# Turning x's tokens with VectorE block transpositions and a DRAM round trip instead of TensorE transposes, in a two-direction Mamba-2 layer

## The reference, cut to what matters

```python
def _mamba2(x, Win, convw, convb, dtb, Alog, Dsk, normw, Wout):
    z, xBC, dt = jnp.split(x @ Win, [D_INNER, D_INNER + CONV_CH], axis=-1)      # 512 | 640 | 8
    xBC = _silu(depthwise causal convolution over 4 tokens of xBC + convb)
    xs, Bm, Cm = jnp.split(xBC, [D_INNER, D_INNER + NGROUPS * D_STATE], axis=-1) # 512 | 64 | 64
    xs = xs.reshape(b, l, NHEADS, HEADDIM)                                       # 8 heads of 64
    dt = jax.nn.softplus(dt + dtb)
    dA = jnp.exp(dt * -jnp.exp(Alog))
    # over the tokens: h = dA_t * h + dt_t * x_t (outer) B_t ;  y_t = C_t . h
    y = ys + Dsk * xs
    y = y * _silu(z)
    y = y * jax.lax.rsqrt(jnp.mean(y * y, axis=-1, keepdims=True) + 1e-05) * normw
    return y @ Wout

def reference(...):
    out = concat(_mamba2(layernorm(x), f...), flip(_mamba2(flip(layernorm(x)), b...))) @ Wo + bo
    x = x + out
    return x + (layernorm(x) @ W.T + b + (layernorm(x) @ V_r) @ C.T)
```

## Time and profile before

| | |
|---|---|
| median of 3 runs | 630.85 us (628.61 to 631.13) |
| span of the profiled execution | 629.0 us |
| median minus that span | 1.85 us |
| PE, DVE, ACT, POOL busy | 592.0, 503.6, 547.2, 409.4 us |
| one period (forward plus reversed scan), seven times | 73.6 us |
| opening up to the first period; after the last | 90.8 us; 23.0 us |

### The profile page before, as it was taken

How to read it: one execution, slowest core, us unless ns; L and a number is a source line. 1 busy time by engine, 2 the same in 40 slices (tenths; PEclk the granted TensorE clock), 3 DMA queues, 4 the chain that set the end, 5 groups by cost and what they waited for, 6 DMA issues and landing times.

```text
span 629.0 us, 13895 instructions
## 1 busy us (share of the span) xinstructions
PE 592.0 (94%) x4320; PEld 461.0 (73%) x4320; DVE 503.6 (80%) x991; ACT 547.2 (87%) x1197; POOL 409.4 (65%) x427
## 2 busy tenths in 40 slices
PE   1998999999999999999999999999999999999995
PEld 1776687777877777777877778777777777777784
DVE  2669788996979879797888969798797978879663
ACT  4689998979999899988999799897999989997952
POOL 1006948787486864878476874868648684768843
PEclk9999999999999999999999999999999999999997
DMA  7533514236061541418132360614416170343500
GB/s 220 189 109 115 198 40 124 92 106 203 8 200 27 171 114 41 169 28 255 28 116 95 107 204 0 211 25 160 126 28 182 26 241 12 92 122 99 181 1 33
DMA packets 43545, 70.71 MB, mean 112 GB/s; under 512 B 8000, under 2 KB 30592, under 8 KB 43520
## 3 DMA queue, kind: packets, MB, share of 16 engines
q1 hardware_dynamic: 43520, 70.40, 36.7%
HBM read 59.37 MB, written 4.72 MB: 102 GB/s over the span
## 4 chain that ended last, share of the span: by engine, by line
PE 55%; ACT 18%; DVE 13%; issue 8%; POOL 3%; SPq 1%; DMA 1%; DVEq 0%; ACTq 0%; POOLq 0%
PE mi L621 14%; ACT bs L968 8%; PE pj L487 7%; PE py L580 7%; PE pj L489 6%; PE pj L488 6%; DVE xc L1378 5%; PE mi L687 4%; PE py L598 3%; ACT bs L974 2%; ACT L953 2%; DVE bs L1405 2%; DVE ss L1437 2%; ACT xc L935 1%; DVE xres L1445 1%
## 5 line engine op out<-in xcount | busy, mean ns | idle before, releaser
L1378 DVE SCALAR_TENSOR_TENSOR xc<-pj,cw,xc 128x510 f32<-128x510 f32 (+2 forms) x240 | 175.4, 744 | 24.9 <-ACT xc L935 23.0
L968 ACT ACTIVATE bs<-bs,s_all 128x128 f32<-128x128 f32 x512 | 158.4, 388 | 0.2
L1892 POOL TENSOR_TENSOR yg<-yg,sz 128x512 f32<-128x512 f32 x60 | 76.9, 1287 | 81.6 <-DVE yg L1424 81.6
L487 PE MATMUL pj<-xnt_hi,w_hi 128*128 128x512 f32 x288 | 126.1, 438 | 0.9 <-DVE xc L1378 0.8
L489 PE MATMUL pj<-xnt_hi,w_lo 128*128 128x512 f32 x288 | 114.2, 396 | 0.0
L488 PE MATMUL pj<-xnt_lo,w_hi 128*128 128x512 f32 x288 | 113.8, 395 | 0.0
L621 PE MATMUL mi<-wc,yg 128*128 128x256 f32 x480 | 112.1, 386 | 0.8 <-DVE xres L1445 0.2
L621 PEld LDWEIGHTS mi<-wc,yg 128*128 128x128 f32 x480 | 88.6, 190 | 16.9 <-issue 3.3
L1405 DVE TENSOR_TENSOR bs<-bs,gm 128x512 f32<-128x512 f32 x128 | 86.1, 680 | 8.5 <-ACT bs L974 7.7
L1871 POOL TENSOR_TENSOR xw<-xdt,w_end 128x512 f32<-128x512 f32 x48 | 49.6, 1045 | 49.8 <-ACT w_end L953 40.9
L1390 DVE TENSOR_TENSOR xdt<-mi,dt 128x512 f32<-128x512 f32 x64 | 42.8, 688 | 44.6 <-PE mi L547 44.2
(11 more groups left out here) (149 smaller groups left out, 1021.6 us busy)
## 6 DMA issues: line engine op xcount, KB each, us to landing
bs<-rows_dram SPq DMA_DIRECT2D x64, 512.0 KB, 5.4
es<-rows_dram SPq DMA_DIRECT2D x128, 96.0 KB, 3.0
xres<-in_x SPq DMA_DIRECT2D x8, 512.0 KB, 3.6
cc<-bcm SPq DMA_DIRECT2D x32, 128.0 KB, 2.3
out<-ot SPq DMA_DIRECT2D x32, 128.0 KB, 3.4
xin<-in_x SPq DMA_DIRECT2D x7, 512.0 KB, 5.3
rows_dram<-s_rows SPq DMA_DIRECT2D x128, 4.0 KB
cz<-bcm SPq DMA_DIRECT2D x16, 128.0 KB, 2.4
```

The lines of the kernel that those rows point to most:

```text
L487: pe.matmul(ps[:], hi(k), xnt_hi[:, k, :], start=(k == 0), stop=False)
L968: i = nc.scalar.activation(bs[:, h, Q * c:Q * c + Q], bs[:, h, Q * c:Q * c + Q], ACT.Relu, bias=s_all[:, d, 0, c, h:h + 1], scale=-1.0)
L1378: i = dve.scalar_tensor_tensor(xc[:, t, to], pj[bank][:, of], cw[:, d, t, KW - 1 - s:KW - s], xc[:, t, to], ALU.mult, ALU.add)
L1892: pool.tensor_tensor(yg[:, d, p, :], yg[:, d, p, :], sz[:, d, p, :], ALU.mult).then_inc(yg_ready, 1)
```

## The change

1. `x_tokens` goes, on TensorE (256 transposes of 128x128) and on VectorE, and with it 64 entries of the tables that share the two `mi` banks.
2. VectorE gets `turn`: for each of the four x tiles of a scan one block transposition of 128x512, which turns each 32x32 block inside its group of 32 partitions and writes to a new buffer `turned`. `xw` now lies in `turned`'s storage.
3. SP gets `scatter` (four DMAs per scan, from `turned` to DRAM, in runs of 2 KB) and `gather` (four per scan, one for each chunk, from DRAM, in runs of 512 B, into `yg`'s storage for that direction). `scatter` waits for all four `turn`s, the first `gather` for all four `scatter`s and for the last head pair of the scan before.
4. VectorE gets `step` in place of its part of `x_tokens`: two instructions of 128x256 per chunk, with both operands (`tok` and `dt`) in SBUF. `intra` of the first pair waits for all four steps; `decayed_x` of a chunk waits for its step.
5. `s_all` is stored by heads, so that `put_rows` and `put_decays` are one DMA each instead of four, and `repeat_decays` is four DMAs per scan instead of eight.
6. The orders of all five lists are new, opening and last scan included.

```diff
+SQ = 32
+BLK = P // SQ
...
+LOOP = ["1bt", "a0", "a1", "dtm", "1s0", "1s1", "0ss", "dtt", "1s2", "0o0", "0o1", "0S", "0ST", "0bt", "1ss", "1o0",
+        "0s0", "0s1", "1o1", "0s2", "1S", "t0", "1ST", "f0", "t1", "t2", "f1", "t3", "f2", "f3"]
...
-        xw = sb("xw", [P, NC - 1, DI])
+        turned = sb("turned", [P, BLK, NC, KI, SQ])
+        xw = turned[:].rearrange("p b c t r -> p (b c t r)")[:, 0:(NC - 1) * DI].rearrange("p (j n) -> p j n", j=NC - 1)
...
+        tok = [yg[:, d].rearrange("p a (b c r) -> p (a b c r)", b=BLK, r=SQ).rearrange("p (b c t r) -> p b c t r", b=BLK, c=NC, t=KI)
+               for d in range(2)]
...
+        tok_dram = nc.dram_tensor("tok_dram", (2, P, BLK, DI), F32, kind="Internal").ap()
...
-                for c in range(NC):
-                    sp.dma_start(rows_dram[d, 0, :, Q * c:Q * c + Q], s_rows[NH * c:NH * c + NH, d, 0, :]).then_inc(rows_stored, 16)
+                sp.dma_start(rows_dram[d, 0].rearrange("h (c q) -> (h c) q", c=NC), s_rows[:, d, 0, :]).then_inc(rows_stored, 16)
+
+            def scatter(b, d):
+                sp.wait_ge(turn_ready, KI * (2 * b + d + 1))
+                alone(sp)
+                for i in range(BLK):
+                    sp.dma_start(tok_dram[d, :, i].rearrange("(q r) n -> r q n", q=BLK),
+                                 turned[SQ * i:SQ * i + SQ].rearrange("r q c t n -> r q (c t n)")).then_inc(tok_stored, 16)
+
+            def gather(b, d, j):
+                if j == 0:
+                    sp.wait_ge(tok_stored, 16 * BLK * (2 * b + d + 1))
+                    alone(sp)
+                    pair_done(b, d, KI - 1)
+                c = ORDER[d][j]
+                sp.dma_start(tok[d][:, :, c].rearrange("p b t n -> p b (t n)"),
+                             tok_dram[d].rearrange("p b (c n) -> p b c n", c=NC)[:, :, c]).then_inc(tok_loaded[j], 16)
...
-            def x_tokens(phase, it, d, j):
-
-                ps, free = misc(phase, it, f"{d}x{j}")
+            def turn(b, d, t):
+
+                u = 2 * b + d
+                dve.wait_ge(xs_ready, KI * u + t + 1)
+                dve.transpose(turned[:, :, :, t, :].rearrange("p b c r -> p c b r"), xs[:, d, t, :]).then_inc(turn_ready, 1)
+
+            def step(b, d, j):
+
+                dve.wait_ge(tok_loaded[j], 16 * (2 * b + d + 1))
+                if j == 0:
+                    dve.wait_ge(dt_ready[d], b + 1)
                 c = ORDER[d][j]
-                dve.tensor_tensor(xdt[:, c, :].rearrange("p (h q) -> p h q", h=NH), ps[:].rearrange("p (h q) -> p h q", h=NH),
-                                  dt[:, d, c, :].unsqueeze(2).broadcast_to([P, NH, HP]), ALU.mult).then_inc(free, 1)
+                of = tok[d][:, :, c].rearrange("p (z a) t r -> p z a t r", z=2)
+                to = xdt[:, c, :].rearrange("p (t z a r) -> p z a t r", z=2, a=2, r=SQ)
+                by = dt[:, d, c, :].rearrange("p (t z) -> p z t", z=2)
+                for z in range(2):
+                    i = dve.tensor_tensor(to[:, z], of[:, z], by[:, z].unsqueeze(1).unsqueeze(3).broadcast_to([P, 2, KI, SQ]), ALU.mult)
+                i.then_inc(step_ready, 1)
```

More of the change, by code:

```diff
@@ L293, in copy_c @@
                 sp.wait_ge(bc_ready, 2 * b + d + 1)
+                if not (isinstance(b, int) and b == d == 0):
+                    sp.wait_ge(gm_full, 2 * b + d)
                 for dst in (cc[0:NS, d, :], cc[NS:P, d, :], cz[0:NS, :]):
@@ L538, in b_tokens @@
                     mm = pe.transpose(ps[:, P * c:P * c + P], bcm[:, d, Q * c:Q * c + Q], ident)
-                mm.then_inc(full, 1)
-            def x_tokens(phase, it, b, d, j):
-                if j == 0:
-                    pe.wait_ge(xs_ready, KI * (2 * b + d + 1))
-                ps, full = misc(phase, it, f"{d}x{j}")
-                c = ORDER[d][j]
-                for t in range(KI):
-                    mm = pe.transpose(ps[:, P * t:P * t + P], xs[:, d, t, Q * c:Q * c + Q], ident)
                 mm.then_inc(full, 1)
@@ L1364, in s_rest @@
                 s_copied(phase, it, d)
-                s, end = (s_all[:, d, i].rearrange("p c h -> p (c h)") for i in range(2))
-                dve.tensor_tensor(wd[:, d], end, s, ALU.subtract).then_inc(wd_ready, 1)
+                s, end = (s_all[:, d, i].rearrange("p h c -> p c h") for i in range(2))
+                dve.tensor_tensor(wd[:, d].rearrange("p (c h) -> p c h", c=NC), end, s, ALU.subtract).then_inc(wd_ready, 1)
             def conv(b, d, t, s):
@@ new lines, in first_scan @@
+                conv(b, 1, 0, 1)
+                norm1_aggr(b + 1, 1)
+                conv(b, 1, 0, 2)
+                conv(b, 1, 0, 3)
+                norm1_bn(b + 1, 2)
+                conv(b, 1, 1, 1)
+                norm1_bn(b + 1, 3)
+                scores(b, 0)
+                norm1_aggr(b + 1, 2)
+                conv(b, 1, 2, 1)
+                conv(b, 1, 1, 2)
+                conv(b, 1, 1, 3)
+                dt_floor(b, 1)
+                conv(b, 1, 2, 2)
+                conv(b, 1, 3, 1)
@@ new lines, in first_scan @@
+                s_copy(phase, it, 1)
+                step(b, 0, 0)
+                conv(b, 1, 2, 3)
+                step(b, 0, 1)
+                conv(b, 1, 3, 2)
+                norm1_aggr(b + 1, 3)
+                s_rest(phase, it, 1)
+                conv(b, 1, 4, 1)
+                state(phase, it, b, 0, 0)
+                conv(b, 1, 4, 2)
+                step(b, 0, 2)
+                conv(b, 1, 3, 3)
+                weights(phase, it, b, 0, 0)
+                step(b, 0, 3)
+                weights(phase, it, b, 0, 1)
@@ L1670, in forward_scan @@
                     norm1_bn(b + 1, 0)
+                dt_value(b, 1)
+                if ahead:
                     norm1_bn(b + 1, 1)
-                x_tokens(phase, it, 0, 0)
-                x_tokens(phase, it, 0, 1)
-                x_tokens(phase, it, 0, 2)
-                x_tokens(phase, it, 0, 3)
-                dt_value(b, 1)
-                scores(b, 0)
-                weights(phase, it, b, 0, 0)
-                state(phase, it, b, 0, 0)
-                conv(b, 1, 0, 1)
-                weights(phase, it, b, 0, 1)
-                squares(phase, it, 1)
-                if ahead:
-                    norm1_bn(b + 1, 2)
-                state(phase, it, b, 0, 1)
+                dt_decay(b, 1)
+                if ahead:
+                    norm1_aggr(b + 1, 0)
+                    norm1_bn(b + 1, 2)
+                conv(b, 1, 0, 1)
                 if ahead:
@@ L1688, in forward_scan @@
                 conv(b, 1, 0, 2)
-                weights(phase, it, b, 0, 2)
-                conv(b, 1, 1, 1)
-                dt_decay(b, 1)
-                state(phase, it, b, 0, 2)
-                if ahead:
-                    norm1_aggr(b + 1, 0)
-                weights(phase, it, b, 0, 3)
-                conv(b, 1, 0, 3)
-                conv(b, 1, 2, 1)
+                dt_floor(b, 1)
+                scores(b, 0)
                 if ahead:
                     norm1_aggr(b + 1, 1)
-                mix(phase, it, last, 1, 0)
+                conv(b, 1, 0, 3)
+                squares(phase, it, 1)
                 if ahead:
@@ L1729, in forward_scan @@
                 conv(b, 1, 3, 3)
+                weights(phase, it, b, 0, 6)
+                turn(b, 1, 0)
+                weights(phase, it, b, 0, 7)
+                conv(b, 1, 4, 1)
                 feed(phase, it, last, 0)
-                conv(b, 1, 4, 1)
-                feed(phase, it, last, 1)
-                outputs(b, 0, 2)
                 conv(b, 1, 4, 2)
                 conv(b, 1, 4, 3)
+                turn(b, 1, 1)
+                turn(b, 1, 2)
+                turn(b, 1, 3)
+                outputs(b, 0, 2)
+                feed(phase, it, last, 1)
+                outputs(b, 0, 3)
                 s_rest(phase, it, 1)
-                outputs(b, 0, 3)
                 feed(phase, it, last, 2)
```

696 lines of the change are left out of this document (344 added, 352 removed).

## The result

The changed kernel takes 695.2 us (median of 4, 692.7 to 702.3), the kernel before 629.9 in the same session: ratio 1.106, 95% interval 1.100 to 1.112 (ratios here, and e1's 688.6 us, are of undisturbed runs alone, so a ratio is not always the quotient of the two medians). I had said 639, range 606 to 662.

What follows compares the result with a forecast made beforehand. TensorE bounds the kernel at 73.6 us a period; after the change VectorE would, at 62.0 + 4.8 + 0.0 + 2.5 + 5.2 = 74.5. Seven periods add 6.3, the last scan 2: 637.3 profiled, median 639 us, range 606 to 662.

Steps and rivals of the forecast that it cites:

- TensorE and ScalarE: Work per period: TensorE loses 4.6 us of transposes and is busy about 67.4 us; ScalarE keeps its 67.2 us.
- Block transpositions: Eight of 128x512 per period on VectorE at 0.60 us each add 4.8 us (2.6 to 9.6).
- the rival that doubles their price: Block transpositions cost twice, 4.8 us more on VectorE, 3.5 net per period: 665 us, chance 0.04.
- Steps and stalls: On VectorE, step halves add nothing net; stalls behind GpSimd instructions add 2.5 us a period (0 to 6.5).
- Seam's gap: VectorE idles 3.1 us where a forward scan ends, before the low half of the normalised input.
- Gathers, 0.6 us a period (0 to 5): At both seams gathers land 9.5 us after the last transposition, just in time against VectorE's roughly 9 us of other work.
- Waits for the convolution, 1.5: VectorE keeps 1.5 of its 2.7 us of waits per period for the convolution.
- Traffic "to some 220" GB/s: DMA traffic rises from 111 GB/s by about 8.4 MB a period to some 220, with room left.
- On TensorE ... I charge nothing: `intra` waits for all four steps, but two states, a projection and old mixes lie in front: no cost.
- Rival "transfers late": Scatter and gather queue with 512 KB loads, 1.5 us more at each seam: 663 us, chance 0.10.
- Opening 0, last scan +2: Outside the seven periods: opening costs 0 (-4 to +5), the last scan +2 us (-2 to +6).
- Faster rival, 613: VectorE needs 71.0 us a period: seam gap 1.5, stalls 0.5, gathers in time; 613 us, chance 0.42.

Runs made afterwards that it cites:

- e1: Changed kernel, but scatters send the input weights' storage and gathers read x, so no gather waits for a scatter: 688.6 us, ratio 1.093.
- e8: Changed kernel without the token scatters and gathers; the steps read x as it stands in SBUF: 635.6 us, ratio 1.007.
- e12: Changed kernel without token transfers and with the steps' second operand from the scores' PSUM bank instead of dt in SBUF: 612.3 us, ratio 0.972.
- e13: Changed kernel, but each scatter sends all 128 partitions instead of 32, same bytes and runs, tokens in another order in DRAM: 670.4 us, ratio 1.064.
- e14: e1 with the four gathers issued ahead of the scatters in both scans: 653.0 us, ratio 1.035.
- e3: Changed kernel plus 12 identity transposes on TensorE ahead of each scan's first and second state: 693.9 us, ratio 1.101.

## Why the prediction was wrong, by its own steps

One more piece of the changed kernel's timeline is used here, the second seam, whose last transposition ends at 320.44:

```profile
326.45 1.29 DVE L1313 TENSOR_TENSOR xnt_lo<-mi,xnt_hi 128x512 fp32r<-128x512 f32 x2 [2.47 <-ACT xnt_hi L915]
327.66 0.69 DVE L1422 TENSOR_TENSOR gm<-gm,cst 128x512 f32<-128x512 f32 x1
331.87 2.50 DVE L1415 TENSOR_TENSOR xdt<-yg,dt 128x256 f32<-128x256 f32 x4 [3.53 <-DMA yg<-tok_dram]
```

- **TensorE and ScalarE**: right in their work. Without late transfers (e8) TensorE is busy 67.8 us a period (I had 67.4), ScalarE 67.0.
- **Block transpositions**: right, 0.60 us and 688 ns each; the rival that doubles their price is out.
- **Steps and stalls**: the mechanism was right, the size somewhat low. VectorE's work falls by 3.45 us a period when the operand leaves SBUF (69.92 in e8, 66.47 in e12), the period by 2.8; I had 2.5 of stalls. In the timeline, where four halves stand in a row, one stall of about 1 us shows: 2.50 us for four, where 4 x 0.33 + 0.1 would be 1.4 (331.87).
- **Seam's gap**: right, up to 2.5 us for ScalarE's high half.
- **Gathers, 0.6 us a period (0 to 5)**: this step failed. Measured are 6.7 us in front of the steps in the period 253 to 335, and 8.0 us longer periods than in e8 (81.0 against 73.0). Both sides of the race were wrong, and neither by much. The trip took 10.8 and 11.4 us where I had 9.5: the scatters' part was put at 5.9 us from loads of 512 KB to all partitions, and from 32 partitions at a time it is 7.6 and 7.2 (with all 128, in e13, 6.2 and 5.2). At the seam from forward to reversed SP's list alone, with its three stores, holds the gather nearly that long. And what VectorE has to do meanwhile was put at 9.1 us; at that seam it is 7.9 with the gap in it (320.44 to the end of the scores at 328.35), at the other 9.4. Then come the steps after the first, each with a gather of its own, which the sum didn't have: the second waits 0.95 us more at 295.03. The wide scatters remove 3.8 of the 8.0 us of a period, the gathers issued early in e14 6.5; how the rest splits is open.
- **Waits for the convolution, 1.5**: there are none in a period of e8 (idle 3.25 us, 2.5 of it the seam's gap), so the period without late gathers came out at 73.0, where my terms give 73.9.
- **Traffic "to some 220" GB/s**: the sum was wrong. The tokens add 33.6 MB to 70.7 in the whole run, 4.2 MB a period and not 8.4 (1 MB out and 1 MB in, twice a period, is 4.2), and the period runs at 151 GB/s.
- **"On TensorE ... I charge nothing"**: wrong with it. The lateness runs on through `xw` to the states (38.0 us of waits; e8 has 10.6), and the clock drops behind them; in e3 the clock came back without a gain clear of noise.
- **Rival "transfers late"** named the mechanism with 0.10 and a condition, over 2 us a scan. It came with 3.5, and its price, 1.5 us a seam, was 4.0 by the periods. The range ended at 662 by that price: its upper end rested on the shape of loads that the scatter doesn't have.
- **Opening 0, last scan +2**: measured 16.4 up to the first mark (which lies 44 us into the first period) and 11.1 behind the last; 5.1 and 5.5 in e8. That the transfers add 11 and 6 us there fits a trip that little work covers. The 5.1 and 5.5 without any transfers are unexplained.
- **Luck**: that e8's 635.6 us stand so close to my sum without the gathers is in part luck. Its six periods are 4.0 us shorter than before, where I had them longer, and its two ends 10.6 longer, where I had 2.
- **Faster rival, 613**: its place was found. It is e12's 612.3, with two of its conditions (no stalls, no waits for gathers) made true by leaving work out. The third, a gap of 1.5 us at the seam, is not met (up to 2.5), so that the two numbers agree to 1 us is chance.

## What to carry to other kernels

Price a DMA by how many partitions of SBUF it touches, not only by its bytes: look in the DMA view for full engines at half the rate, and if the blocks must be narrow try alternating the partition halves 0 to 63 and 64 to 127 (17 us of 695 here). Count the issues too: sixteen small DMAs took the queue's engine 10.1 us. A queue is a line, and so is the list of the engine that issues: a transfer that depends on nothing can still be held up by all that stands ahead of it, so an edit that cuts only the dependence may show next to nothing. And a trip through DRAM in front of the bound engine needs cover of its full length at each seam, or the rest is added once per scan.

## What was not expected of the hardware

- 1 MB from SBUF to DRAM went at about 200 GB/s in DMAs of 32 partitions, 317 to 484 GB/s in DMAs of 128, with the same runs of 2 KB; the order 0, 2, 1, 3 of four narrow DMAs is worth 17 us of 695.
- SP's issue of such a DMA took 319 ns at best and 2152 at worst.
- TensorE's granted clock fell to the lower level (1.2 of 2.4 GHz: starts 0.43 us apart instead of 0.23) during some 9 us (mean granted clock there 0.66) behind two waits of 1.7 and 1.35 us at the states; keeping the engine busy with idle transposes brought the mean to 0.983, without a gain in time.
